# A macaron layer on one core: the first steps of the second expert network, with half of b1 loaded at the end of the scores, the first slot tile transposed ahead of the last sums, the last router group spread over more steps, and b2 of 16 tiles added by GpSimd

## The reference, cut to what matters

```
x = x + 0.5 * ffn(layernorm(x))        # x: 16 x 256 rows of 128
x = x + attention(layernorm(x), context)
x = x + 0.5 * ffn(layernorm(x))

def ffn(x):                            # 8 experts, each row goes to one
    top = argmax(x @ gate_w.T + gate_b + expert_bias)
    for e in range(8):
        h = relu(x @ w1[e] + b1[e])    # 128 -> 512
        y = h @ w2[e] + b2[e]          # 512 -> 128
        out += (top == e) * y
```

## Time and profile before

| | |
|---|---|
| median of three runs | 758.66 us (757.59 to 760.12) |
| the profiled execution's own time | 754.72 us |
| its span | 752.9 us |
| busy: PE, DVE, ACT, POOL | 95%, 80%, 66%, 47% |
| mean granted TensorE clock | 0.984 of full speed |

### The profile page before, as it was taken

The page is one execution under the profiler, slowest core; times in us unless marked ns, Lnnn a source line. Parts: engine busy times, 40 slices in busy tenths (PEclk is TensorE's granted clock), DMA queues, the critical chain, the costliest instruction groups (busy, mean ns, idle before and its releaser), DMA issues.

```text
span 752.9 us, 15236 instructions
## 1 busy us (share of the span) xinstructions
PE 716.0 (95%) x4374; PEld 600.2 (80%) x4374; DVE 604.1 (80%) x1659; ACT 496.9 (66%) x1211; POOL 357.5 (47%) x486
## 2 busy tenths in 40 slices
PE   9979999799999999999999999999999999789993
PEld 7759888678888888878888878887887887569992
DVE  6979899887787878788788888787878877588883
ACT  3676777577677677767667767767766765446661
POOL 4055787243333345446346345444534533266663
PEclk9989999999999999999999999999999999999997
DMA  9931433200000000000000000000000011222210
GB/s 251 346 131 40 97 89 75 73 1 1 1 1 1 1 8 8 1 2 15 0 1 15 2 1 12 5 0 4 12 1 1 15 43 53 103 77 66 58 50 10
DMA packets 31792, 31.49 MB, mean 42 GB/s; under 512 B 5049, under 2 KB 26183, under 8 KB 31200
## 3 DMA queue, kind: packets, MB, share of 16 engines
q1 hardware_dynamic: 27360, 23.91, 10.6%
q0 software_dynamic: 3520, 6.40, 3.2%
q10 hardware_dynamic: 832, 0.21, 0.1%
HBM read 20.96 MB, written 10.47 MB: 42 GB/s over the span
## 4 chain that ended last, share of the span: by engine, by line
PE 71%; DVE 13%; DMA 5%; issue 4%; POOL 2%; ACT 1%; DVEq 1%; SPq 0%; POOLq 0%; ACTq 0%
PE bank L1403 15%; PE bank L1405 15%; PE bank L1404 15%; PE bank L1612 13%; DMA x_packed<-slot_rows 4%; PE bank L1450 3%; DVE neg_max L1291 3%; DVE probsT_lo L1297 2%; PE bank L1438 2%; DVE hT_lo L1151 2%; PE bank L1453 1%; DMA b<-in_L_ffn_b 1%; POOL rows L549 1%; PE bank L1352 1%; PE bank L1653 1%
## 5 line engine op out<-in xcount | busy, mean ns | idle before, releaser
L565 POOL TENSOR_SCALAR probs<-probs,row_inv 128x512 f32<-128x512 f32 x256 | 177.6, 694 | 274.5 <-DVE row_inv L1302 273.3
L754 ACT ACTIVATE probs<-bank,neg_max 128x512 f32<-128x512 f32 x256 | 176.1, 688 | 144.1 <-DVE neg_max L1291 142.9
L1291 DVE TENSOR_REDUCE neg_max<-bank 128x1 f32<-128x512 f32 x256 | 176.4, 689 | 86.9 <-PE bank L1405 84.3
L1297 DVE TENSOR_TENSOR probsT_lo<-bank,probsT_hi 128x512 fp32r<-128x512 f32 x256 | 174.1, 680 | 2.1 <-ACT probsT_hi L763 2.0
L1612 PEld LDWEIGHTS bank<-ident,probs 128*128 128x128 f32 x1024 | 127.3, 140 | 37.0 <-issue 1.7
L1612 PE MATMUL bank<-ident,probs 128*128 128x128 f32 x1024 | 153.4, 272 | 0.5 <-DVE probsT_lo L1297 0.3
L763 ACT ACTIVATE probsT_hi<-bank 128x512 fp32r<-128x512 f32 x256 | 150.8, 589 | 2.1 <-PE bank L1612 2.1
L1403 PE MATMUL bank<-m_hi,xT_hi 128*128 128x512 f32 x256 | 122.3, 478 | 1.5 <-ACT probs L754 1.5
L1403 PE MATMUL bank<-probsT_hi,vw_hi 128*128 128x512 f32 x256 | 101.7, 397 | 4.2 <-DVE probsT_lo L1297 4.2
L1404 PE MATMUL bank<-probsT_lo,vw_hi 128*128 128x512 f32 x256 | 101.5, 396 | 0.0
L1405 PE MATMUL bank<-probsT_hi,vw_lo 128*128 128x512 f32 x256 | 101.5, 396 | 0.0
(11 more groups left out here) (219 smaller groups left out, 1240.3 us busy)
## 6 DMA issues: line engine op xcount, KB each, us to landing
b<-in_L_ffn_b SPq DMA_DIRECT2D x4, 1024.0 KB, 7.0
x_packed<-slot_rows SPq DMA_DIRECT2D x39, 65.5 KB
slot_rows<-slots SPq DMA_DIRECT2D x39, 65.5 KB, 1.8
x_stats<-rows SPq DMA_DIRECT2D x4, 524.0 KB, 10.2
rows<-x_packed SPq DMA_DIRECT2D x8, 262.0 KB, 3.0
rows<-in_L_attn_x SPq DMA_DIRECT2D x4, 512.0 KB, 8.3
w_lo<-in_L_ffn_w SPq DMA_DIRECT2D x8, 256.0 KB, 7.2
w_hi_lo<-in_L_ffn_w SPq DMA_DIRECT2D x8, 256.0 KB, 5.4
```

The costliest lines, as they stand in the source:

```text
L565: pool.tensor_scalar(PR[:, u % 4, :], PR[:, u % 4, :], RI[:, u % 4:u % 4 + 1], 1.0, ALU.mult, ALU.mult).then_inc(normed, 1)
L754: act.activation(PR[:, n % 4, :], BK[n % 2][:, :], ACT.Exp, bias=NM[:, n % 4:n % 4 + 1], accum_out=SU[:, n % 4:n % 4 + 1]).then_inc(probs, 1)
L1291: v.tensor_reduce(NM[:, n % 4:n % 4 + 1], BK[n % 2][:, :], AX.X, ALU.max, negate=True)\
L1297: v.tensor_tensor(PTL[at], BK[2 + u % 2][:, :].rearrange("p (c q) -> p c q", c=KC), PTH[at].bitcast(fp32), ALU.subtract).then_inc(pT_lo, 1)
```

## The change

What it does: SP issues the first half of b1 as soon as the last scores are done. PE transposes slot tile 0 between the sums of unit 251 and those of unit 252, and ACT takes its high part and norms tile 1 before it evacuates the last group's sums (`o_evac`). In steps 1 and 2 PE does the router part behind the w1 matmuls instead of ahead of the slot transpose, in banks 6 and 7 instead of 0 and 1. Halving b2 goes from DVE to ACT (step 1). The adds of b2 for tiles 0 to 15 go from DVE to POOL, one at the head of each of its steps 0 to 15. DVE reads the tile's expert register ahead of the router part in steps 1 to 16. RANK_STEP is 7 instead of 6, and the one-hot chain of eight small DVE instructions takes three steps (3, 3, 2) instead of two (5, 3). Nothing else moves; the work is the same.

```diff
-        ROW_STEP, STAT_STEP, LOGIT_STEP, RANK_STEP = 1, 2, 4, 6
+        ROW_STEP, STAT_STEP, LOGIT_STEP, RANK_STEP = 1, 2, 4, 7
+        B2_FIRST = 16
...
             sp.wait_ge(scores, UNITS)
+            load_b1(0)
             sp.wait_ge(pT_ps, UNITS)
-            load_b1(0)
             load_b1(1)
...
+            def add_b2(j):
+                if j == 0:
+                    pool.wait_ge(bias_half, 2)
+                pool.wait_ge(s_xn, SLOTS + j + 1)
+                e = expert(pool, j)
+                row = XS[:, j % R, 0:D].unsqueeze(1)
+                apart(pool, pool_passed)
+                pool.tensor_tensor(row, row, B2S[1][:, ds(e, 1), :], ALU.add).then_inc(s_xb_first, 1)
...
             def step(m):
+                if m < B2_FIRST:
+                    add_b2(m)
                 if live(m, 5) and m - 5 < CLOSE:
                     add_low(1, m - 5)
...
+            def half_b2():
+                act.wait_ge(b2_in, 16 * 2)
+                act.activation(B2S[1], B2S[1], ACT.Copy, scale=0.5).then_inc(bias_half, 1)
...
-                    if r == 1 and m == STAT_STEP:
+                    if r == 1 and m == STAT_STEP - 1:
+                        half_b2()
+                    if r == 1 and m == STAT_STEP + 1:
                         x2T_evac(NG - 1)
...
                 slot_norm(0)
+                step(0)
                 if r == 1:
                     o_evac(NG - 1)
-                tiles(step, 5)
+                tiles(step, 5, 1)
...
-                        e = expert(dve, j)
+                        e = loaded.pop(j) if j in loaded else expert(dve, j)
...
-                    if r == 1 and m == 1:
-                        half_b2(1)
-                    if r == 1:
+                    if r == 1 and 0 < m < EARLY:
+                        loaded[m - 1] = expert(dve, m - 1)
                         last_group(m)
...
-                if m == LOGIT_STEP:
-                    onehot(g, range(5))
-                if m == LOGIT_STEP + 1:
-                    onehot(g, range(5, 8))
+                if LOGIT_STEP <= m < RANK_STEP:
+                    onehot(g, range(3 * (m - LOGIT_STEP), min(3 * (m - LOGIT_STEP) + 3, 8)))
...
-            rounds(slot)
+            step = experts(1)
+            for n in range(UNITS + LAG_AV - G):
+                slot(n)
             pe.wait_ge(routed, 2)
-            experts(1)
+            step(0)
+            for n in range(UNITS + LAG_AV - G, UNITS + LAG_AV):
+                slot(n)
+            tiles(step, 4, 1)
```

More of the change, by code:

```diff
@@ L263, in macaron_kernel @@
         LATE = SLOTS - EARLY
-        ROW_STEP, STAT_STEP, LOGIT_STEP, RANK_STEP = 1, 2, 4, 6
+        ROW_STEP, STAT_STEP, LOGIT_STEP, RANK_STEP = 1, 2, 4, 7
+        B2_FIRST = 16
         EMPTY_LINKS, EARLY_LINKS = 12, 13
         def router_bank(g, step=0):
-            return (step - 1) % 2 if g == NG - 1 else RANK_BANK
+            if g < NG - 1:
+                return RANK_BANK
+            return 5 + step if step <= STAT_STEP else (step - 1) % 2
         def rounds(slot):
@@ L290, in ahead, with tiles @@
             return after(n, s, -1)
-        def tiles(step, lags):
-            for m in range(SLOTS + lags):
+        def tiles(step, lags, first=0):
+            for m in range(first, SLOTS + lags):
                 step(m)
@@ L1046, in m_low, with half_b2 @@
                     .then_inc(m_lo, 1)
[L1048 to L1050 removed]
+            def half_b2():
+                dve.wait_ge(b2_in, 16)
+                v.tensor_scalar(B2S[0], B2S[0], 0.5, None, ALU.mult).then_inc(bias_half, 1)
             gate_weights()
@@ L1077, in _ @@
                 w1_low(e)
-            half_b2(0)
+            half_b2()
             w2_low(0)
@@ L1120, in experts @@
             def experts(r):
+                own_b2 = B2_FIRST if r else 0
+                loaded = {}
                 def step(m):
                     if m == 2:
+                        dve.wait_ge(b1_in, 32 * (r + 1))
+                    if m == own_b2 + 2:
                         dve.wait_ge(bias_half, r + 1)
-                        dve.wait_ge(b1_in, 32 * (r + 1))
                     if r == 1 and m == EARLY + 2:
@@ L1135, in step @@
                                         B1[:, ds(e, 1), :], ALU.add).then_inc(s_hb, 1)
-                        row = XS[:, j % R, 0:D].unsqueeze(1)
-                        v.tensor_tensor(row, row, B2S[r][:, ds(e, 1), :], ALU.add).then_inc(s_xb, 1)
+                        if j >= own_b2:
+                            row = XS[:, j % R, 0:D].unsqueeze(1)
+                            v.tensor_tensor(row, row, B2S[r][:, ds(e, 1), :], ALU.add).then_inc(s_xb, 1)
                     if live(m, 5):
@@ L1141, in step @@
                         dve.wait_ge(s_ylo, SLOTS * r + j + 1)
-                        dve.wait_ge(s_xb, SLOTS * r + j + 1)
+                        if j < own_b2:
+                            dve.wait_ge(s_xb_first, j + 1)
+                        else:
+                            dve.wait_ge(s_xb, SLOTS * r + j + 1 - own_b2)
                         v.scalar_tensor_tensor(out=row, in0=BK[6 + j % 2][:, 0:D], scalar=0.5, in1=row,
@@ L1455, in step @@
                         last.then_inc(s_y, 1)
-                    if r == 1:
+                    if r == 1 and m > STAT_STEP:
                         last_group(m)
@@ L1467, in step @@
                         head_rest(BEFORE_FFN + m)
+                    if r == 1 and m <= STAT_STEP:
+                        last_group(m)
                     if r == 0 and m == SLOTS + 2:
@@ L1470, in step @@
                         xn_transposes(0, 1)
-                tiles(step, 4)
+                return step
             def last_group(m):
```

14 lines of the change are left out of this document (5 added, 9 removed).

## The result

The changed kernel took **750.86 us** (median of 4 runs, 747.89 to 751.46) against 759.39 for the kernel before beside it (757.59 to 765.86): ratio 0.9874, 95% interval 0.9843 to 0.9904. On the 758.66 us of the prediction that is 749.1. The sign was right and the time was not: 752.9 forecast, and the lower end of the range, 750.2, was still 1.1 too high.

What follows compares the result with a forecast made beforehand. Bound by a PE hole at the hand-over from attention, then steps 0.8 us longer than PE needs, then steps PE fills. Terms -3.4 - 2.3 - 1.8 + 1.7 = -5.8 from 758.66 gave 752.9 us, range 750.2 to 756.8.

Steps and rivals of the forecast that it cites:

- What bounds the kernel: Three stretches: a hole after attention, steps 0.8 us longer than PE needs, then steps that PE fills by itself.
- A: Start: early b1 and b2 no longer awaited by DVE bring step 2's h add from 646.46 to 643.1, -3.4 us.
- Hidden: Tile 12's load, asked for at 664.7, leaves ACT's norm up to 0.7 us late, covered by PE's later use.
- B: Steps 2 to 4: three steps at 2.45 us each, 7.35 in all where before took 9.63: -2.3 us.
- C: Steps 5 to 11: shorter DVE steps by router part, 18.45 us where before took 20.26: -1.8 us.
- The rival that the load only moves: DVE's register load is not hidden, 0.31 us more in each of ten steps: 755.3 us; chance 0.12.
- D: POOL from step 8: b2 adds at 0.70 us each make ACT wait for the low add by step 17: +1.7 us.
- rival 1: POOL keeps up: a b2 add costs 0.45 us, no lateness from POOL: 751.2 us; chance 0.14.
- The sum: Whole change: -3.4 - 2.3 - 1.8 + 1.7 = -5.8 us, giving 752.9 us from 758.66.
- rival 5: POOL takes it all: a b2 add costs 1.5 us or more, time from 758.9 us up; chance 0.04.
- Rival 3: Router's two-input DVE instructions in steps 8 to 11 collide with a full POOL, +1.5 us half covered: 753.7; chance 0.12.
- Rivals 4 and 5: 4: the hole at the start stays, 756.3 us, chance 0.07; 5: POOL takes it all, from 758.9 up, chance 0.04.

Runs made afterwards that it cites:

- the fills later: Changed kernel with the eight fills of the regions' tails issued behind the loads of tiles 12 to 14, not ahead of them: 746.96 us, ratio 0.9894.
- the load at the add: Changed kernel with the expert's register loaded just before the h add again, as before the change: 752.64 us, ratio 0.9866.
- the old spread: Changed kernel with the router's steps spread as before the change (one-hot in 5 and 3, ranks in step 6): 746.47 us, ratio 0.9896.
- the combined kernel: Changed kernel with fills behind loads of tiles 12 to 14, only 10 tiles' b2 adds on GpSimd, b2's halving behind tile 0's relu: 756.14 us, ratio 0.9926.
- one sort a step: Changed kernel with GpSimd's four last-group sorts issued one in each of steps 8 to 11, not two in steps 8 and 9: 746.99 us, ratio 0.9888.

## Why the prediction was wrong

**What bounds the kernel**, and **A**: right. t(2) 2.27 against 2.35 forecast (-3.4 us, as forecast). Its cover was underpriced, though: a late b2, with 3.07 us of ACT's waiting, costs 6.4 us, where I wrote a us for a us. **Hidden**: right as well. In the changed kernel on chip C ACT waits 1.34 us for tile 12's load ahead of the wait for L523 of 1.27; with the fills later it is one wait of 2.74 for L523.

**B**: right. t(2) to t(5) 7.25, forecast 7.35.

**C**, steps 5 to 7: 7.06 in the five kernels with the new spread that had neither pauses nor a low clock there (7.24 to 7.29 in the changed kernel on A and D and in the first result), forecast 7.65. The gap ahead of the h add is 0.14, not 0.25: the load is hidden nearly whole. The rival that the load only moves is refuted by its own experiment (0.56 with the load at the add).

**D is the step that failed**, and in it one number: "I take 0.70, half of the load hidden". Register loads and adds of POOL on chip C (min/median/max ns):

```profile
L324 POOLq TENSOR_LOAD <-expert_of_tile x16: 284/288/513, 641.3 to 674.5; - x16
...
L591 POOL TENSOR_TENSOR slot_rows<-slot_rows,b x16: 407/444/495, 642.1 to 677.0; 128x128 f32<-128x128 f32 x16
```

```profile
667.88 1.01 POOL L602 DMA_INDIRECT out<-slot_rows  x1 [0.17 <-POOL slot_rows L523]
668.89 0.48 POOL L591 TENSOR_TENSOR slot_rows<-slot_rows,b 128x128 f32<-128x128 f32 x1
669.30 0.44 POOL L523 TENSOR_TENSOR slot_rows<-slot_rows,y_lo_half 128x128 f32<-128x128 f32 x1
```

While POOL is behind, its b2 add starts as the scatter ahead of it ends (668.89), and its low add 0.41 later: nothing of the load's 0.29 shows. My chain put the end of add_low of tile 10, and with it t(17), at t(8) + 1.7 + 11.5 + 5.1 + 7b. With b = 0.70 that is t(8) + 23.2, with b = 0.41 it is t(8) + 21.2. Measured: 21.1 to 21.2 in six profiles without pauses, each with all 16 adds on GpSimd, the new spread and two sorts a step (21.0 with the old spread). On chip C the chain itself can be read: add_low of tile 3 ends at 658.42 and that of tile 10 at 677.83, 19.41 later, which is 11.5 + 5.1 + 7 x 0.41. The whole miss at t(17), 37.7 for 40.55 (9.49 + 7.06 + 21.15), is 0.2 by A and B, 0.6 by C's early steps and 2.05 by 7b. I had nearly the value in hand as the lower bound, 0.45 from a row of the same shape, and left the load half visible, though rival 1 says that DVE's queue hides such loads. **Rival 1** (b = 0.45) was the right case: it gives 17.35 + 21.45 = 38.8.

C and D are also not two terms. POOL's chain from t(8) on sets the pace up to t(17), so the 1.0 us by which C's steps 8 to 11 came out shorter than forecast (9.8 for 10.8) gave nothing. What is left of D once b is 0.41 is small: without the seven adds t(17) comes only 0.4 to 0.5 us earlier.

**The sum** against undisturbed profiles: t(17) from 45.92 (46.45 in the profile that I forecast from) to 37.7, -8.2 us, where I had -5.8. The 37.7 is put together from stretches; the kernel with the fills later, which has all of them, measured 37.81. The changed kernel's own profiles on C and E have 39.3, since their clock fell in step 5 (last section). The times there say -9.7 (chip C) and -7.9 (E); what lies between these and 8.2 I can't resolve. So the price b explains 2.05 of the 2.85 us that are missing at t(17); for the 3.8 us by which the time itself was off, the rest stays open. In the first result the pauses make the changed kernel's profile 2.3 us longer at t(17) and 2.5 more behind it (19.2 us from the last h add to the end, 16.7 without pauses), and before's 759.39 lies 4 above its level on B, C and E as well. I had set the 3.9 us between before's profile and its median down as a constant; the runs show that the level moves by up to 8 us between chips and the ratio hardly.

Two small sums in the prediction are off and carry nothing: by its terms tile 12 is asked for at 664.9, not 664.7, and rival 5 starts at 758.7, not 758.9.

**Rival 3**, collisions: not in the forecast's size, and the mechanism is real. L993 took 0.50 before, and 0.50 again on chip B. On a chip without pauses it meets a sort of POOL after the change and no longer its low add (chip C, first row); in the first result, where the pauses shift it, it meets the low add again (second and third):

```profile
666.49 0.26 DVE L1016 SCALAR_TENSOR_TENSOR block_of_tile<-tile_f,early_blocks,tile_index 128x22 int32<-128x22 f32 x1
667.14 0.51 DVE L1016 SCALAR_TENSOR_TENSOR block_of_tile<-tile_f,early_blocks,tile_index 128x22 int32<-128x22 f32 x1
667.15 0.44 POOL L523 TENSOR_TENSOR slot_rows<-slot_rows,y_lo_half 128x128 f32<-128x128 f32 x1
```

This instruction takes 0.26 or 0.27 in the seven profiles where a sort is being issued beside it, 0.24 with POOL idle (the combined kernel), and 0.46 to 0.51 in the six where the low add starts with it. By the port rule of the Trainium skill (SBUF — State Buffer, "Who interferes with whom") a two-input VectorE instruction and a GpSimd instruction that reads SBUF exclude each other: the trace agrees for the low add beside it (0.50 on chip B), and the issue of a sort beside it costs this instruction 0.03 at most. In the changed kernel on chip C steps 8 to 11 show none of the rival's 1.5 us. With one sort a step, though, 1.7 us came, as shown above: where GpSimd's work falls beside the router's decides it, and the rival's price took no account of that. **Rivals 4 and 5** didn't occur; the wait on L523 came, 0.2 to 1.3 us a step in the changed kernel in place of "up to 2" (2.7 once with the fills later).

**Left open:** what ACT's pauses are. Shown: they come on two chips of five and in the first result, and neither ACT's place in its program nor the fills move the first one. Not shown: that the sorts belong to them, and how before looks with them.

## What to carry to other kernels

When one engine is behind over several steps, its own chain sets the end: price that chain alone, and don't add what other engines save inside it. A register load was nearly free here wherever earlier work of its engine stood ahead of the instruction that needs it (0.41 us for load and add together on GpSimd, a gap of 0.14 for 0.56 on VectorE), so price such an instruction by the start-to-start time of its like in a backlog. Work that moves to GpSimd can lengthen VectorE's instructions that run beside it; look at what will lie side by side. And price a transfer awaited ahead of TensorE's work not by its lateness but by what the pause does to the clock behind it; here, moving the consumer behind the first relu made the order of the loads indifferent.

## What the runs showed of the hardware

The clock can also fall behind a much shorter lack of work. In two of the changed kernel's profiles (chips C and E) the step from t(5) to t(6) takes 3.4 and 3.7 us instead of 2.23. Windows of the one on chip E:

```profile
648.00:650.00 2.00, 1.19 (x8) 0.77 (x8) 1.97 (x8) 1.40 (x5) 1.64 (x4) 1.00 0.03 6
650.00:652.00 2.00, 2.00 (x19) 1.89 (x18) 1.17 (x2) 0.43 (x2) 0.37 (x1) 0.94 0.00 0
652.00:655.00 3.00, 3.00 (x14) 2.70 (x13) 2.21 (x7) 1.26 (x4) 0.87 (x2) 0.50 0.00 0
```

PE was busy 1.19 of 2 us, then fully, and only then ran at 0.50. In the first profile of the changed kernel it was busy 1.16 of the same 2 us, and the clock stayed at 1.00:

```profile
642.20:644.20 2.00, 1.16 (x8) 0.75 (x7) 1.97 (x7) 1.35 (x5) 1.78 (x4) 1.00 0.03 6
644.20:646.20 2.00, 2.00 (x19) 1.95 (x18) 1.23 (x3) 0.44 (x2) 0.43 (x2) 1.00 0.00 0
646.20:649.20 3.00, 3.00 (x24) 2.67 (x23) 2.63 (x9) 2.09 (x7) 0.87 (x2) 1.00 0.00 0
```

Up to t(5) the profiles of this kernel agree (t(2) to t(5) 7.22 to 7.31, but 7.71 on chip C), and three of the five show no fall in step 5: the same work sometimes costs 1.2 to 1.4 us more.

The same program has two levels by chip, 745.6 to 747.4 and 751.2 to 751.9 us, and the records of ACT show part of the difference as pauses, the first of them 2.47 to 2.60 us long in all seven profiles of A, D and the first result that have GpSimd's b2 adds.
